# A two-layer graph network on one core: softmax and aggregation of the first two edge blocks placed among the later gathers, gathers of 128 rows

## What is computed

```
# layer 0: spline convolution, mean over a destination's edges
h = relu(layernorm(x)); x1 = x + segment_mean(messages(h[src], edge_attr), dst) + h @ root_w.T + root_b
# layer 1: graph attention with self loops, 8 heads of 32
h = relu(layernorm(x1)); xp = (h @ W_gat).reshape(N, 8, 32)
alpha = leaky_relu(a_src[src] + a_dst[dst], 0.2)       # edges and self loops
ea = exp(alpha - segment_max(alpha)[dst]); attn = ea / (segment_sum(ea)[dst] + 1e-16)
h1 = segment_sum(xp[src] * attn, dst).mean(heads) + bias_gat
h2 = layernorm(h1 + h) * g1 + be1
out = x1 + layernorm(relu(h2 @ w1 + b1) @ w2 + b2 + h2) * g2 + be2
```

## Time and profile before

| | |
|---|---|
| three runs | 3395.88, 3396.81, 3410.65 us (median 3396.81) |
| profiled execution | 3399.81 us, its span 3398.0 us |
| mean granted TensorE clock | 0.773 of full speed |
| POOL busy | 2533.3 us, 75% |
| PE busy | 2270.3 us, 67% |
| DVE busy | 1842.4 us, 54% |
| ACT busy | 862.2 us, 25% |

### The profile page before, as it was taken

The page is one execution under the profiler, slowest core; times in us unless marked ns, Lnnn a source line. Parts: engine busy times, 40 slices in busy tenths (PEclk is TensorE's granted clock), DMA queues, the critical chain, the costliest instruction groups (busy, mean ns, idle before and its releaser), DMA issues.

```text
span 3398.0 us, 34863 instructions
## 1 busy us (share of the span) xinstructions
PE 2270.3 (67%) x10329; PEld 1608.8 (47%) x10329; DVE 1842.4 (54%) x3167; ACT 862.2 (25%) x1636; POOL 2533.3 (75%) x2011
## 2 busy tenths in 40 slices
PE   2886777747777777777777475566561587887750
PEld 1554455535555555565555354445440244454430
DVE  4788878883433434333333232322248998797730
ACT  1332222212333232322323122222221122222220
POOL 7788888887887878787777787887840038888877
PEclk9888888877888787777877676676665798787775
DMA  2322222221111112121111111111100001111100
GB/s 57 85 70 70 68 71 65 48 63 31 33 38 35 38 37 41 36 41 35 38 27 32 26 24 24 24 27 20 23 16 0 30 15 29 32 26 28 33 10 10
DMA packets 116073, 123.70 MB, mean 36 GB/s; under 512 B 70597, under 2 KB 72618, under 8 KB 115941
## 3 DMA queue, kind: packets, MB, share of 16 engines
q0 software_dynamic: 64000, 30.57, 9.4%
q1 hardware_dynamic: 51940, 91.52, 8.4%
HBM read 59.51 MB, written 64.00 MB: 36 GB/s over the span
## 4 chain that ended last, share of the span: by engine, by line
POOL 65%; issue 19%; DVE 8%; PE 7%; DMA 0%; DVEq 0%; ACT 0%; POOLq 0%; ACTq 0%
POOL ring L409 44%; POOL x_table L431 14%; POOL out_rows L457 6%; DVE region L1457 2%; PE V L773 1%; PE C L525 1%; PE V L513 1%; DVE region L1449 1%; DVE region L1123 1%; DVE region L1433 1%; DVE region L1385 0%; PE C L773 0%; DVE region L1408 0%; DVE region L1405 0%; PE C L519 0%
## 5 line engine op out<-in xcount | busy, mean ns | idle before, releaser
L409 POOL DMA_INDIRECT ring<-in_x,index x800 | 1042.6, 1303 | 244.3 <-issue 244.0
L457 POOL DMA_INDIRECT out_rows<-ring,index_out x400 | 510.0, 1275 | 370.3 <-DVE ring L1264 250.6
L1092 DVE TENSOR_REDUCE var<-sq 125x16 f32<-125x512 f32 x325 | 220.4, 681 | 839.9 <-ACT sq L838 734.9
L409 POOL DMA_INDIRECT ring<-x_table,index x400 | 492.0, 1230 | 124.4 <-issue 124.1
L431 POOL DMA_INDIRECT x_table<-region,index_out x400 | 485.7, 1214 | 121.9 <-issue 121.9
L838 ACT ACTIVATE sq<-C 125x512 f32<-125x512 f32 x300 | 179.4, 598 | 961.9 <-PE C L525 416.5
L513 PE MATMUL V<-xT,w_q 128*128 128x500 f32 x600 | 365.3, 762 | 53.5 <-ACT xT L830 25.7
L474 PE MATMUL T<-ident,hrow 125*128 125x125 f32 x1000 | 196.3, 335 | 194.4 <-DVE hrow L1108 171.8
L525 PEld LDWEIGHTS C<-w_c,hid 128*125 128x125 f32 x2400 | 320.1, 219 | 0.0
L525 PE MATMUL C<-w_c,hid 128*125 128x32 f32 x2400 | 319.4, 296 | 0.0
L489 PE MATMUL C<-center,xT 128*125 128x128 f32 x1400 | 258.6, 347 | 78.5 <-DVE hrow L1114 47.2
(11 more groups left out here) (223 smaller groups left out, 3421.6 us busy)
## 6 DMA issues: line engine op xcount, KB each, us to landing
ring<-in_x,index POOLq DMA_INDIRECT x800
nodes<-in_x SPq DMA_DIRECT2D x25, 500.0 KB
x_table<-nodes SPq DMA_DIRECT2D x25, 500.0 KB
x_plain<-nodes SPq DMA_DIRECT2D x25, 500.0 KB
nodes<-x_plain SPq DMA_DIRECT2D x50, 250.0 KB
out_rows<-nodes SPq DMA_DIRECT2D x50, 250.0 KB
x_table<-region,index_out POOLq DMA_INDIRECT x400
ring<-x_table,index POOLq DMA_INDIRECT x400
```

Source lines behind the costliest of these rows:

```text
L409: pool.indirect_dma_start(out=ring[0:P, j, s * F:(s + 1) * F], out_offset=None, in_=table, in_offset=bass.IndirectOffsetOnAxis(ap=index[0: ...
L457: pool.indirect_dma_start(out=out[:, :], out_offset=bass.IndirectOffsetOnAxis(ap=index_out[0:P, j, s:s + 1], axis=0), in_=ring[0:P, j, s * ...
L1092: v.tensor_reduce(unit(var, k), slots(squares(k)), AX.X, ALU.add).then_inc(var_ready, 1)
```

## The change

The softmax is split at the end of block 1 (EARLY = 2 blocks, 160 of 400 columns). It is done for the first part in D, after turns 10 (scan of the maximum and join over rows), 11 (merge, subtraction, exp, scans of the sum) and 12 (second join, weights). After each of the turns 13 to 22 the x part of one chunk of blocks 0 and 1 follows (`x_early`), with V in two banks, since D uses the other two. The segment that may go on from block 1 into block 2 is not complete then: its part in the first blocks is summed apart (`open_sums`, 16 matmuls a chunk of 8 x 32 results, weights `alpha_open`), and when its maximum and sum are known it is scaled and multiplied into the carry of block 2. `y_first` replaces the lone x block: output rows of block 0, interleaved with the softmax of blocks 2 to 4 (240 columns). Then e_block(2, 1), (3, 2), (4, 3), (none, 4). Loops of PE, ACT and DVE over blocks in D and E are written out. `softmax_done` no longer holds SP. The staging copy of `diff` on ACT (L967) is gone: PE transposes from `diff` itself. The 400 gathers from the table of updated rows take 128 partitions; the three additional index rows come from one load at the start, and their results are not used.

```diff
+EARLY = 2
+E1 = EARLY * P * SE
+X_FROM = NJ * EARLY + 3
+FIRST_JOIN, SECOND_JOIN = (2, 3), (5, 6)
+X_END = (4, 7, 8, 9, 10)
...
+        alpha_open = region2[:, 2 * H * TE + H * EARLY * SE:2 * H * TE + 2 * H * EARLY * SE].rearrange("p (h t) -> p h t", h=H)
+        open_end = region2[:, 12500:12500 + EARLY * SE]
...
+            sp.dma_start(index[P:128, :, :], src[0:(128 - P) * SE].rearrange("(p j s) -> p j s", p=128 - P, j=NJ)).then_inc(fill_in, 16)
...
+            load(last_i[0:P, :], dst[E1 - 1:E1].rearrange("(a f) -> a f", a=1).to_broadcast([P, 1]), ends_in)
...
-            sp.wait_ge(softmax_done, 1)
...
-            def gather(table, j):
+            def gather(table, j, rows=P):
                 pool.sem_inc(cleared, 1)
                 for s in range(CE):
                     pool.indirect_dma_start(
-                        out=ring[0:P, j, s * F:(s + 1) * F], out_offset=None, in_=table,
-                        in_offset=bass.IndirectOffsetOnAxis(ap=index[0:P, j, s:s + 1], axis=0)).then_inc(ring_dma[j], 16)
-
-            def gather_phase(table, phase, used):
...
-            gather_phase(x1_table[0:N, :], 2, 2)
+            pool.wait_ge(fill_in, 16)
+            gather_phase(x1_table[0:N, :], 2, 2, 128)
...
+            def open_sums(c):
+
+                at, bank = cq.next()
+                pe.wait_ge(c_done, cq.room)
+                for i in range(CE):
+                    e = c * CE + i
+                    m = mm(C[bank][0:H, 0:F], alpha_open[0:P, :, e], diff[0:P, e * F:(e + 1) * F],
+                           start=i == 0, stop=i == CE - 1, skip_group_check=True)
+                m.then_inc(c_ready, 1)
+
...
+            def x_early(c):
+                if c == 0:
+                    pe.wait_ge(softmax_done, 1)
+                t = transpose(diff[0:P, c * W:(c + 1) * W])
+                open_sums(c)
+                for g in range(G):
+                    x_values(t, EARLY_T[c % 2], g, V)
+                if c == NJ - 1:
+                    x_tail_T(X_END[0])
+                    x_carry_T(X_END[0])
+
+            tq.restart(); cq.restart(); fq.restart(); vq.restart()
+            fq.depth, vq.depth = 2, 2
+            pe.wait_ge(f_done, 4 * NU * NB + CREDIT)
+            for b in range(NB):
+                for w in range(NJ):
+                    d_turn(b, w, first=b + w == 0)
+                    at = b * NJ + w
+                    if at == X_FROM - 3:
+                        ends_T(EARLY, FIRST_JOIN[0])
+                        carries_T(EARLY, FIRST_JOIN[0])
+                    if at == X_FROM - 2:
+                        ends_T(EARLY, FIRST_JOIN[1])
+                    if at == X_FROM - 1:
+                        carries_T(EARLY, FIRST_JOIN[1])
+                    if X_FROM <= at < X_FROM + EARLY * NJ:
+                        x_early(at - X_FROM)
+            d_turn(None, None, last=True)
+
+
+            tq.restart(); cq.restart(); vq.restart(); fq.restart()
+            tq.depth, cq.depth, vq.depth = 1, 1, 4
...
+            def y_first():
+                late = NB - EARLY
+                ends_T(late, SECOND_JOIN[0])
+                t = y_rows(0, 0)
...
+                at, bank = tq.next()
+                pe.wait_ge(t_done, tq.room)
+                pe.wait_ge(open_ready, 1)
+                nc.tensor.transpose(T[bank][0:F, 0:H], open_scaled, ident[0:H, 0:H]).then_inc(t_ready, 1)
+                at, bank = cq.next()
+                pe.wait_ge(c_done, cq.room)
+                pe.wait_ge(t_done, tq.at + 1 + CREDIT)
+                for h in range(H):
+                    i = mm(C[bank][0:F, 0:1], gat_bd[0:F, h * GF:h * GF + F], open_T[:, h:h + 1], start=h == 0, stop=h == H - 1)
+                i.then_inc(c_ready, 1)
+            y_first()
+
...
+            pe.wait_ge(softmax_done, 2)
+            for y in range(1, NB):
+                e_block(y + 1 if y + 1 < NB else None, y)
...
+            def y_first():
+                late = NB - EARLY
+                y_square(0, 0)
+                ends_rows(late)
+                root(2)
+                affine()
+                y_square(0, 1)
+                hidden()
+                carries_rows(late)
+                root(2); square(3); affine(); root(3)
+                exps(EARLY, late, 1)
+                act.wait_ge(ratio_ready, 1)
+                nc.scalar.activation(ratio, gap, ACT.Exp).then_inc(exp_ready, 1)
+                nc.scalar.activation(own_in, max_in, ACT.Exp, scale=-1.0).then_inc(exp_ready, 1)
+                y_square(0, 2)
+                hidden()
+                root(2); square(3); affine(); root(3)
...
+            def x_early(c):
+                at, rows = bank_ready()
+                if c == 0:
+                    v.tensor_copy(open_sum, rows[0:H, 0:F]).then_inc(c_done, 1)
+                else:
+                    dve.wait_ge(c_done, at + CREDIT)
+                    v.tensor_tensor(open_sum, open_sum, rows[0:H, 0:F], ALU.add).then_inc(c_done, 1)
+                pending = []
+                x_products(c, 0, pending, V)
+                x_products(c, 1, pending, V); x_sum(c, pending)
+                x_products(c, 2, pending, V); x_sum(c, pending)
+                x_products(c, 3, pending, V); x_sum(c, pending); x_sum(c, pending)
+                if c == NJ - 1:
+                    x_tail(0)
+                    x_carry(0)
+                    x_on(0)
+
+            cq.restart(); steps.restart(); vq.restart(); rq.restart()
+            vq.depth = 2
+            for b in range(NB):
+                for w in range(NJ):
+                    d_turn(b, w, first=b + w == 0)
+                    at = b * NJ + w
+                    if at == X_FROM - 3:
+                        for j in range(NJ):
+                            dve.wait_ge(rows_landed[j], NB * DMAS)
+                            dve.wait_ge(x1_saved[j], 16 * NB)
+                        for k in range(2):
+                            dve.wait_ge(base_saved[k], 16 * NB * (3 - k))
+                        to_segments(slots_of(self_logit, 0, EARLY), 0, EARLY)
+                        join_rows(0, EARLY, ALU.max, FIRST_JOIN[0], max_in)
+                    if at == X_FROM - 2:
+                        join_slots(slots_of(self_logit, 0, EARLY), 0, EARLY, ALU.max, FIRST_JOIN[0])
+                        below_max(0, EARLY)
+                        denominators(0, EARLY, 0)
+                    if at == X_FROM - 1:
+                        join_rows(0, EARLY, ALU.add, FIRST_JOIN[1], sum_in)
+                        join_slots(denom_of(EARLY), 0, EARLY, ALU.add, FIRST_JOIN[1])
+                        weights(0, EARLY, 0)
+                        v.tensor_tensor(alpha_open[0:P, :, :], slots_of(beta, 0, EARLY), open_end[0:P, :].unsqueeze(1).to_broadcast([P, H, EARLY * SE]),
+                                        ALU.mult).then_inc(softmax_done, 1)
+                    if X_FROM <= at < X_FROM + EARLY * NJ:
+                        x_early(at - X_FROM)
+            d_turn(NB, 0, last=True)
+
+
...
+            def y_first():
+                late = NB - EARLY
+                own, other = slots_of(self_logit, EARLY, late), denom_of(late)
+                y_sum(0, 0)
+                to_segments(own, EARLY, late)
+                y_norm(0, spread(2))
+                y_sum(0, 1)
+                join_rows(EARLY, late, ALU.max, SECOND_JOIN[0], max_in)
+                whole_first(late, ALU.max, total)
+                step(v.tensor_tensor(gap, total, max_in, ALU.max))
+                step(v.tensor_tensor(gap, max_in, gap, ALU.subtract))
+                y_norm(1, spread(2))
+                y_finish(0, 0, spread(3))
+                join_slots(own, EARLY, late, ALU.max, SECOND_JOIN[0])
+                below_max(EARLY, late)
+                dve.sem_inc(ratio_ready, 1)
+                y_sum(0, 2)
+                y_norm(2, spread(2))
+                y_finish(0, 1, spread(3))
+                denominators(EARLY, late, 3)
+                y_sum(0, 3)
+                dve.wait_ge(exp_ready, 8)
+                step(v.scalar_tensor_tensor(out=sum_out, in0=own_in, scalar=1e-16, in1=sum_in, op0=ALU.add, op1=ALU.add))
+                step(v.tensor_tensor(sum_out, sum_out, ratio, ALU.mult))
+                v.tensor_tensor(own_in, own_in, ratio, ALU.mult)
+                step(v.tensor_tensor(sum_in, sum_in, ratio, ALU.mult))
+                join_rows(EARLY, late, ALU.add, SECOND_JOIN[1], sum_in)
+                whole_first(late, ALU.add, total)
+                step(v.scalar_tensor_tensor(out=total, in0=own_in, scalar=1e-16, in1=total, op0=ALU.add, op1=ALU.add))
+                step(v.reciprocal(total, total))
+                step(v.tensor_tensor(total, total, sum_out, ALU.mult))
+                v.tensor_scalar(open_scaled, open_sum, total, None, ALU.mult).then_inc(open_ready, 1)
+                y_norm(3, spread(2))
+                y_finish(0, 2, spread(3))
+                join_slots(other, EARLY, late, ALU.add, SECOND_JOIN[1])
```

(26 more changed lines are left out.)

522 lines of the change are left out of this document (280 added, 242 removed).

## The result

The changed kernel took 3547.6 us (median of 4 runs, 3540.1 to 3558.2) against 3401.1 before on the same chip: ratio 1.043, 95% interval 1.039 to 1.047. It is slower by 4.3%, where 3300 us and 3230 to 3385 were forecast. The runs behind this showed that the number has two values: on another occasion the same code took 3269 us, ratio 0.962 [0.959, 0.965].

A forecast was written before the change was run, and what follows sets the result against it. POOL's queue of indirect DMAs plus its 248.8 us pause was taken as the bound. Stage work to 2602, 138 and 52 us to 2792, 20 chunks (505) to 3297 and 3 to the end gave 3300 us; range 3230 to 3385.

The forecast's parts named there:

- The gather: Updated-row gathers, 125 to 128 rows: 1.0 us each (bounds 0.39 and 1.24), 21.1 us a chunk of 16.
- The rival with an unchanged gather: Gathers of updated rows stay at 1.21 us, turn 10 starts 38 us later: 3338 us; chance 0.22.
- A plain turn of 18.8 us: Updated-source gather stage: a turn, the steps over one edge chunk, costs 18.8 us without its wait for gathers.
- The slower rival: In-order turns do not overlap: aggregation at 26 us a chunk in turns 13 to 22, 3420 us; chance 0.10.
- turns 40 us apart: Sign that the forecast is wrong; turns 13 to 22 were expected about 33 us apart.
- the 2740 that was to show the forecast wrong: First scatter of updated edge rows after 2740 us means wrong; 2600 to 2670 was expected.
- Softmax of two blocks, 44 us: Turns 10 to 12, softmax of blocks 0 and 1: 44 us together, nothing allowed to overlap.
- Aggregation, 14 us a chunk and 10 for a scan: Blocks 0 and 1 in turns 13 to 22: 14 us added per chunk, plus 10 for block 0's scan.
- First output block: After the stage's vector work ends at 2602: 33 us to the first scatter at 2635, 138 us of DVE work.
- Sum: Whole kernel: 3300 us span, 3302 as profiled time, median 3299, given as 3300 us, -2.8%; chance 0.56.
- One rival's sum: Everything hides better: x work 8 us, gather 0.8 or less, 3240 us; with gather 0.39, 3199; chance 0.12.
- At nothing: Extra start loads, written-out loops, the removed ACT staging copy and SP's missing softmax wait were taken to cost nothing.

The follow-up runs named there:

- after_third: The changed kernel, byte for byte the one of the result, measured once more on another occasion: 3269.0 us, ratio 0.962.
- after_g125: The changed kernel with its 400 gathers of updated rows back at 125 rows, nothing else changed: 3314.5 us, ratio 0.976; measured again, 3320.0 us, ratio 0.977.
- before_g128: The kernel before the change with only the 128-row gathers in that stage and the load of the three extra index rows: 3521.4 us, ratio 1.036.
- gather_rows_again: Separate measurement without the kernel's computation: 60 TensorE units beside 64 gathers in each of 16 stages, varying row counts and memsets: 1.30 us a unit everywhere.
- gather_rows_third: gather_rows_again unchanged, on another occasion: while the gathers ran, TensorE finished 7 of 60 units at 128 rows, all 60 at 125.

## Why the prediction was wrong

Wrong in its sign in the condition of the result. Where TensorE isn't slowed the time came inside the range and 1% off, in part because errors cancel, as told below. Point by point, the steps' numbers against after_third's trace:

- **The gather**: 1.0 us and 21.1 a chunk were forecast; 0.96 to 0.99 came in both conditions, and chunks of 19.9 to 21.0 us where POOL didn't wait. The bounds from 0.39 to 1.24 held. The rival with an unchanged gather fell.
- **A plain turn of 18.8 us**, and with it the stage. *This is the step that failed.* It was worked out as turns less waits for gathers, and then used with gathers that follow each other after 1.25 us in place of 1.53, as though TensorE's own time did not depend on them. In the trace of the result turns 2 to 10 cost 28 us each (2082.4 to 2308.5), after the one that took 124. In after_third turns 0 to 10 stand 204.4 us apart in all with 25.6 of it waits for gathers, so 17.9 each. That turn 10 began at 2135.0, as forecast to the microsecond, is luck: the first gather came 8 us later than assumed (1909.1, not 1901.1) and eleven chunks went 0.8 us faster each (20.3, not 21.1).
- **No rival held this.** The slower rival had turns that don't overlap, and its sign would have been "turns 40 us apart". Turns 13 to 22 were 26 to 62 us apart, with a mean of 39, and the first scatter came at 2874.6, after the 2740 that was to show the forecast wrong; the cause was none of those listed.
- **Softmax of two blocks, 44 us**: turns 10 to 12 took 86.6 us in after_third, 33 more than three plain ones. **Aggregation, 14 us a chunk and 10 for a scan**: turns 13 to 22 took 302.8, which is 124 more than ten plain ones, against 150. The terms were too high by 11 and 26 us. In the first the items were priced right: DVE took 9.5 us for the 24 scans, 12.0 for the eight passes of mask and merge, 1.6 for the subtractions and 8.2 for the reciprocal, against 9.5, 11.2, 1.5 and 8.1. (The 0.40 us a scan was right, though "half way" between 0.23 and 0.90 would be 0.57.) DVE's softmax work comes to 39 us and the turns grew by 33, so some of it lay beside the turns' own waits, where the forecast let nothing overlap. For the aggregation it stays open which item was too dear. Turn 24 began at 2543.8 against 2582.
- **First output block**: turn 24 to the first scatter took 52.7 us, forecast 53 (20 + 33). The rows of the second block came 172 us after the first scatter, forecast 157, POOL starving in three bits of 10.1, 5.7 and 18.8 us, where four were forecast (the fourth place has 0.5 us, hardly over the 0.3 of issue). From there 20 chunks took 509 us, forecast 508.
- **Sum**: span 3277 against 3300, of which the stage is 38 us too high and the first output block 15 too low. In the condition of the result the span is 279 us longer. One rival's sum doesn't come out of the forecast's own terms: with turns of 18.8 us, turn 10 would begin 26 us earlier with a gather of 0.8 us and 33 earlier with one of 0.39, so that rival stands for 3214 and 3207 us, not 3240 and 3199.
- **At nothing**: the written-out loops cost 0.2% alone, close to that.
- **The page's two rules**: the split over 16 engines that the Trainium skill (DMA: Bandwidth & Descriptors, on why a DMA increments its semaphore by 16) gives for 128 rows agrees with the trace, 16 packets of 1024 B a gather. The same page's small cost for making descriptors (Anatomy of one DMA), by which the instruction would have stayed at 1.21 us, doesn't agree: it fell to 0.94.

What remains open: why TensorE's completions come late (whether its matmuls run late or are only reported late, the modelled ends can't tell), and what sets a chip's condition. On five occasions the slowness was there and on four it wasn't, all kernels of an occasion agreeing; two occasions minutes apart with the same chip number differed, so the chip's number doesn't settle it. Whether other work on the chip at that time has a part in it wasn't looked at. No other stage of this kernel issues so fast. The scatters of the last stage, 1.49 us apart, did no harm: from the first scatter to the end it took 681.8 us in the slowed run and 680.5 in the other. Scatters at 1.25 us and plain DMAs weren't tried.

The version to keep, if the condition can't be chosen, is after_g125: 3314.5 us on the occasion on which before_g128 was slowed and 3320.0 on one without the slowness. Pacing 128 rows with one memset gave 3313.0 and 3361.8, so it buys nothing over 125 rows. The change as made is 1.5% faster than after_g125 in the one condition and 7% slower in the other.

## What to carry to other kernels

A transfer that gets cheaper also comes more often; before counting on that, ask what its pace does to the engines that only share the chip with it, and put a rival for it into the sum even if the trace of before has nothing to price it with. When waits end on "remote" while the engine that should have ended them stands idle in the trace, suspect that its completions are late, and measure it alone with the suspect work switched on and off. And when two measurements contradict each other, run them together on one chip before building a theory on their difference: two kernels here went into a difference that was none of the programs'.

## What the runs showed of the hardware

- In some conditions of a chip, indirect DMAs issued every 1.18 to 1.33 us slow TensorE from 1.3 us for a unit of four small fp32 transposes and four products to 33.6 (2.8 for each of its twelve matmul instructions in the trace), with ScalarE and VectorE unharmed (0.59 us a copy at either end of such a wait). At 1.44 us over half is lost, at 1.52 an eighth, from 1.60 nothing. In other conditions none of it shows (1.30 us a unit in every stage of gather_rows_again).
- In gather_rows_third the first two or three units of a stage are still fast, and in the stages of up to 1.25 us all but 112 rows reach 33.6 us a unit 22 to 35 us after the first; the first copy behind the last gather came 3 to 12 us later, without memsets (stage of 128 rows: copies at 283.8, 286.3, 287.6, 290.5, 297.6, 318.7, 352.3, 373.3; gathers from 283.3 to 365.5, then copies 0.5 to 2.5 us apart at first).
- The instruction's length goes with the rows as follows (us): 32 rows 0.87, 64 0.91, 96 0.92, 112 0.94, 128 0.95, 120 0.99, 126 1.00, 100 1.01, 121 1.03, 125 1.21, 124 1.29, 127 2.55. The prime number among them, 127, costs most.
- Beside 125-row gathers a slowed chip costs a dense TensorE an eighth (gather_rows_third), and yet the complete kernel with 125 rows took 3314.5 us in such a condition and 3320.0 in the other: that stage has slack for it.
